# Transposing the routed tokens on VectorE, in blocks of 32, instead of on TensorE

## The chip, the core and the metric

The kernel runs on one core of one Trainium2 chip. The metric is the device time of one execution in microseconds. Three executions of the kernel before took 958.41, 960.04 and 960.34 us; the median is 960.04 us.

## What is computed

There are 4096 tokens (64 x 64) with 512 features each. First every token goes through a conditioning layer: `h = cond_w[itok].T @ x + fside[itok]`, where `itok` names one of 8 subjects for each group of 64 tokens. The reference then computes a mixture of experts on `h`:

- logits `h @ gate_weight.T` over 16 experts, sigmoid, a bias, the best 2 of 4 groups, the best 4 experts of those, and their scores normalized and scaled by 2.5 as weights `w`;
- for each chosen expert `y = silu(h @ gate.T) * (h @ up.T) @ down.T`, with 512 features in and out and 256 hidden ones, added with its weight `w`;
- one shared expert of the same shape for every token, with weight 1;
- the result is `x` + the routed sum + the shared output, all in float32.

## The kernel before, in words

**Tiles.** Work is cut into tiles of 128 tokens (one token per partition). There are NT = 32 tiles of all tokens for the shared expert, and then NR = 143 routed tiles: the (token, expert) pairs sorted by expert, each expert padded to whole tiles. The tile number n runs from 0 to 174 through one software pipeline over both kinds; LAST is 174.

**Stages.** First 32 tiles are conditioned (TensorE, line 697), stored as rows of `h_rows` in HBM and their logits are made (lines 707 to 714). VectorE computes the routing from them beside this stage and beside the 32 shared tiles. Then the 143 routed tiles run. Most of them are in a hardware loop (`run_tiles`, line 90), which is unrolled 16 times; a head and a tail stand outside it.

**Precision.** A float32 product is made of three products in the type fp32r: the operand's high part times the weights' high part, high times low, and low times high (`split_product`, line 770). ScalarE makes a high part by a copy (lines 583, 589 and 608), and VectorE the low part by subtracting it (lines 1204, 1209 and 1236).

**One routed tile n.** GpSimd gathers 128 rows of `h_rows` into a slot of `tok_ring` (line 490); the 8 slots hold 512 features and the token's 16 expert weights. TensorE transposes the features, four blocks of 128x128, into the PSUM bank `psT[n % 2]` (`xpose`, line 747). ScalarE copies that into `xT_hi` (line 583), and VectorE makes `xT_lo` (line 1204). TensorE does the gate and up product, 12 matmuls of 512 columns, into `psGU` (`gate_up`, line 779). ScalarE applies Silu (line 636), and VectorE multiplies by the up half and the expert's weight (`mix`, line 1221). TensorE transposes the hidden values, two blocks, into `psH` (`xpose_hid`), which are split in the same way (lines 589 and 1209), and does the down product, 6 matmuls of 512 columns, into `psY` (`down`, line 787). ScalarE copies this to a slot of `y_ring`, of which there are 4 (line 598). GpSimd adds the rows into `out` by an indirect DMA that accumulates (line 495).

**The order on each engine in pipeline step n.** It is written out by hand, and every engine works in order:

- TensorE: transposes of x of tile n+1, gate and up product of n, hidden transposes of n-1, down product of n-2.
- ScalarE: `copy_y` of n-3, `copy_xT` of n+1, Silu of n, `copy_hidT` of n-1, then up to three pieces of the next expert's weights (line 608).
- VectorE: `split_x` of n+1, `mix` of n, `split_hid` of n-1, then the weights' pieces (line 1236).
- GpSimd: for routed tile r, the gather of r+9 once `mix` has freed its slot, then the scatter of r once SyncE has allowed it.
- SyncE (SP), in its own step n: where the expert table says so, it starts the load of a next expert's weights (1.5 MB, line 380); then it waits until y of n is copied (line 407), waits for earlier scatters where the expert changes (line 411), and allows the scatter (line 412). It runs about three steps behind TensorE, since y of n is copied in ScalarE's step n+3.

**The rings.** `x_ring` (8 slots of 128x512) holds the input of the conditioning stage, and later tables of the routing; in the routed stage it is not used. The expert weights come with their k axis laid out so that feature `k * 128 + p` lies on partition p (`columns`, line 1341).

Of the kernel before, what the change touches and what calls it, by code (L numbers as in the profile page):

```python
# [14 lines left out]
P = 128  # L15
B, C, H = 64, 64, 512
N = B * C
NT = N // P
# [15 lines left out]
YRING = 4  # L34
AHEAD = 9
PAD_SETS = 4
PADS = PAD_SETS * P
# [67 lines left out]
def build(nc, x, itok, fside, cond_w, gate_w, expert_bias, ffn_w, out):  # L105
# [4 lines left out]
    with ExitStack() as ctx:  # L110
# [6 lines left out]
        def sem(name):  # L117
            return ctx.enter_context(nc.semaphore(name))
# [182 lines left out]
        dve_clear = sem("dve_clear")  # L301
        xposed = sem("xposed")
        xT_ready = sem("xT_ready")
        gu_done = sem("gu_done")
# [10 lines left out]
        TURNS = (NR - RING) // (2 * RING) * 2  # L315
        FFN = (0, NT + NR - RING * TURNS - 1, TURNS, 1)
        LAST = NT + NR - 1

# [16 lines left out]
        def is_shared(n):  # L335
            return n is not None and n < NT
# [4 lines left out]
        def _(sp):  # L341
# [35 lines left out]
            def load_raw(turn, odd):  # L377
# [4 lines left out]
                             ).then_inc(raw_loaded, 16)  # L382

            def shared_step(t, n):
                if n in RAW_LOADS:
                    turn = RAW_LOADS[n]
                    if turn == 1:
                        sp.wait_ge(order_ready, 1)
                    else:
                        sp.wait_ge(low_done, PIECES * (turn - 1))  # L390
                        sp.wait_ge(raw_loaded, 16 * (turn - 1))
                    load_raw(turn, turn % 2)
                if n + RING - 1 < NT:
                    load_h(n + RING - 1)
# [18 lines left out]

            def step(t, n, j):
                if is_shared(n):
                    shared_step(t, n)
                else:
                    if n == NT:
                        sp.wait_ge(sp_words_ready, 1)
                    routed_step(t, n)  # L420

            run_tiles(sp, *FFN, step)

# [111 lines left out]
        def _(act):  # L535
# [43 lines left out]
            def copy_xT(t, n):  # L579
                act.wait_ge(xposed, t.done(1))  # L580
                if n is None or n >= 2:
                    act.wait_ge(gu_done, t.done(-1))
                act.activation(xT_hi[:, t.slot % 2, :], psT[t.slot % 2][:], ACT.Copy).then_inc(xhi_ready, 1)  # L583
# [74 lines left out]
        def _(pe):  # L658
# [88 lines left out]
            def xpose(t, n):  # L747
                if is_shared(n):
                    pe.wait_ge(h_loaded[t.slot], (t.rnd + 1) * 16)
                else:  # L750
                    pe.wait_ge(gathered[t.slot], (t.rnd - (NT // RING - 1)) * 16)
                if n is None or n >= 2:
                    pe.wait_ge(xT_ready, t.done(-1))
                transposes(psT[t.slot % 2], tok_ring[:, t.slot, 0:H], HK).then_inc(xposed, 1)
# [57 lines left out]
            def step(t, n, j):  # L812
# [5 lines left out]
                kept.append(at)  # L818
                if n is None or n < LAST:
                    xpose(t + 1, None if n is None else n + 1)  # L820
                gate_up(t, n, kept[-1], needed)
# [22 lines left out]
        def _(v):  # L844
# [357 lines left out]
            def split_x(t):  # L1202
                v.wait_ge(xhi_ready, t.done(1))
                v.tensor_tensor(xT_lo[:, t.slot % 2, :], psT[t.slot % 2][:], xT_hi[:, t.slot % 2, :].bitcast(F32),  # L1204
                                ALU.subtract).then_inc(xT_ready, 1)

            def split_hid(t):
                v.wait_ge(hidhi_ready, t.done(1))
                v.tensor_tensor(hidT_lo[:, t.slot % 2, :], psH[:, 0:I], hidT_hi[:, t.slot % 2, :].bitcast(F32),  # L1209
                                ALU.subtract).then_inc(hidT_ready, 1)  # L1210
# [81 lines left out]
            def step(t, n, j):  # L1292
# [7 lines left out]
                if n is None or n < LAST:  # L1300
                    split_x(t + 1)
                if is_shared(n):
                    route_part(n)
# [25 lines left out]
            split_x(tile_at(0))  # L1329
            run_tiles(v, *FFN, step)  # L1330
            split_hid(tile_at(LAST))


# [34 lines left out]
```

## Time and profile before

| what | value |
|---|---|
| median of three runs | 960.04 us |
| the profiled execution's own time | 958.84 us |
| its span (first to last instruction) | 957.0 us |
| TensorE matmul busy | 935.2 us (98%) |
| VectorE busy | 411.6 us (43%) |
| ScalarE busy | 399.7 us (42%) |
| GpSimd busy | 432.1 us (45%) |
| mean granted TensorE clock | 0.991 |
| queue q0 (GpSimd's DMAs), time of its packets | 50.0% of 16 engines |
| queue q1 (SP's DMAs), time of its packets | 15.3% of 16 engines |

The profiled execution is one run under the hardware profiler. A share of the span is an average over stages with different limits. Matmuls overlap in this view (each is shown for 0.39 us, though the next begins 0.23 us later), so that the length of a stretch is better read from the chain of waits, which is the work that ended last, followed back. A DMA queue's share is the time that its packets took, over all 16 DMA engines.

### The profile page before, as it was taken

What the parts mean: (1) busy time and instruction counts of PE and PEld (TensorE: products, weight loads), DVE (VectorE), ACT (ScalarE), POOL (GpSimd) and SP (SyncE); (2) the same over time, 40 slices, a digit from 0 to 9 for tenths busy, and PEclk for the clock granted to TensorE, in tenths of its full rate; (3) what the DMA queues carried; (4) which work ended last, traced back from release to release, by engine and by line L of the source; (5) the groups of instructions that cost most, each with busy time, mean ns of one, the idle gap of its engine ahead of it and who ended that gap; (6) DMA issues with size and microseconds to landing.
All of it is one profiled execution on the core that took longest, in us unless ns stands there. A gap on an engine that the chain in (4) does not pass through costs nothing.

```text
span 957.0 us, 21289 instructions
## 1 busy us (share of the span) xinstructions
PE 935.2 (98%) x4822; PEld 762.0 (80%) x4823; DVE 411.6 (43%) x930; ACT 399.7 (42%) x852; POOL 432.1 (45%) x402
## 2 busy tenths in 40 slices
PE   7999999999999999999999999999999999999994
PEld 4777887888888888788888888888888878888883
DVE  1375667776343333443234423534435344343331
ACT  3664333443443333443335433534435344344331
POOL 4330211113355555465465555545554646555533
PEclk9998999999999999999999999999999999999997
DMA  7978686867786666577565866686866858666644
GB/s 230 346 242 259 144 170 165 242 119 198 171 187 113 109 114 113 99 201 162 108 119 107 238 122 111 125 232 114 209 146 159 201 94 190 114 112 114 110 66 56
DMA packets 54465, 149.15 MB, mean 156 GB/s; under 512 B 7434, under 2 KB 7442, under 8 KB 51986
## 3 DMA queue, kind: packets, MB, share of 16 engines
q0 software_dynamic: 37296, 86.95, 50.0%
q1 hardware_dynamic: 15586, 50.12, 15.3%
q10 hardware_dynamic: 1408, 10.49, 3.2%
q14 instruction: 155, 1.27, 0.4%
q8 instruction: 20, 0.33, 0.1%
HBM read 90.87 MB, written 65.04 MB: 163 GB/s over the span
## 4 chain that ended last, share of the span: by engine, by line
PE 95%; issue 2%; ACT 0%; POOL 0%; DMA 0%; DVE 0%; DVEq 0%; POOLq 0%; ACTq 0%; SPq 0%
PE psGU L775 50%; PE psY L775 25%; PE psT L672 9%; PE psH L672 4%; PE psY L697 3%; PE psGU L713 3%; PE psM L801 1%; POOL out L495 0%; DMA cond_sb<-cond_w 0%; DVE xT_lo L1204 0%; ACT split_w L608 0%; PE psM L725 0%; POOLq L476 0%; ACT xT_hi L583 0%; PE psM L682 0%
## 5 line engine op out<-in xcount | busy, mean ns | idle before, releaser
L775 PE MATMUL psGU<-split_w,xT_hi 128*128 (+1 forms) x1400 | 450.8, 403 | 2.4 <-DVE xT_lo L1204 2.4
L495 POOL DMA_INDIRECT out<-y_ring,idx_all x143 | 231.0, 1615 | 275.0 <-SPq L412 269.5
L775 PEld LDWEIGHTS psGU<-split_w,xT_hi 128*128 128x128 f32 x1400 | 251.6, 190 | 48.1 <-issue 2.7
L775 PE MATMUL psGU<-split_w,xT_lo 128*128 (+1 forms) x700 | 275.8, 394 | 0.0
L775 PE MATMUL psY<-split_w,hidT_hi 128*128 (+1 forms) x700 | 232.9, 414 | 0.5 <-issue 0.5
L636 ACT ACTIVATE aT<-psGU 128x256 f32<-128x256 f32 x175 | 67.4, 385 | 344.3 <-PE psGU L775 344.3
L1204 DVE TENSOR_TENSOR xT_lo<-psT,xT_hi 128x512 fp32r<-128x512 f32 x175 | 120.8, 690 | 196.6 <-ACT xT_hi L583 195.1
L598 ACT ACTIVATE y_ring<-psY 128x512 f32<-128x512 f32 x175 | 103.9, 594 | 152.6 <-PE psY L775 126.5
L1221 DVE SCALAR_TENSOR_TENSOR aT<-aT,tok_ring,psGU 128x256 f32<-128x256 f32 x143 | 68.8, 481 | 227.5 <-ACT aT L636 227.5
L490 POOL DMA_INDIRECT tok_ring<-h_rows,idx_all x143 | 145.6, 1018 | 46.2 <-issue 42.3
L775 PEld LDWEIGHTS psGU<-split_w,xT_lo 128*128 128x128 f32 x700 | 132.0, 189 | 28.9
L775 PE MATMUL psY<-split_w,hidT_lo 128*128 (+1 forms) x350 | 138.9, 397 | 0.0
L672 PEld LDWEIGHTS psT<-ident,tok_ring 128*128 128x128 f32 x828 | 104.2, 142 | 41.8 <-issue 16.8
L775 PEld LDWEIGHTS psY<-split_w,hidT_hi 128*128 128x128 f32 x700 | 118.6, 189 | 16.7 <-issue 1.0
L672 PE MATMUL psT<-ident,tok_ring 128*128 128x128 f32 x828 | 125.6, 275 | 0.3 <-ACT scores L570 0.3
L583 ACT ACTIVATE xT_hi<-psT 128x512 fp32r<-128x512 f32 x175 | 103.7, 593 | 1.5 <-PE psT L672 1.4
L504 POOL DMA_DIRECT2D out<-y_ring x32 | 27.6, 862 | 153.1 <-ACT y_ring L598 153.1
L775 PEld LDWEIGHTS psY<-split_w,hidT_lo 128*128 128x128 f32 x350 | 65.7, 188 | 14.5
L1209 DVE TENSOR_TENSOR hidT_lo<-psH,hidT_hi 128x256 fp32r<-128x256 f32 x175 | 73.1, 418 | 1.0 <-ACT hidT_hi L589 1.0
L1236 DVE TENSOR_TENSOR split_w<-raw_w,split_w x42 | 51.5, 1226 | 48.8 <-ACT split_w L608 48.3
L589 ACT ACTIVATE hidT_hi<-psH 128x256 fp32r<-128x256 f32 x175 | 66.5, 380 | 1.4 <-PE psH L672 1.4
L672 PEld LDWEIGHTS psH<-ident,aT 128*128 128x128 f32 x350 | 48.6, 139 | 23.0 <-DVE aT L1221 0.4
(170 smaller groups left out, 470.8 us busy)
## 6 DMA issues: line engine op xcount, KB each, us to landing
raw_w<-ffn_w SPq DMA_DIRECT2D x17, 1536.0 KB, 8.2
h_rows<-tok_ring SPq DMA_DIRECT2D x32, 256.0 KB, 3.5
tok_ring<-h_rows SPq DMA_DIRECT2D x32, 256.0 KB, 4.0
out<-y_ring POOLq DMA_DIRECT2D x32, 256.0 KB, 4.6
x_ring<-x SPq DMA_DIRECT2D x24, 256.0 KB, 4.0
tok_ring<-h_rows,idx_all POOLq DMA_INDIRECT x143, 4.4
out<-y_ring,idx_all POOLq DMA_INDIRECT x143, 4.9
x_ring<-x ACTq DMA_DIRECT2D x8, 256.0 KB, 3.7
```

Source lines behind the costliest of these rows:

```text
L490: pool.indirect_dma_start(tok_ring[:, r % RING, :], None, h_rows[:, :], bass.IndirectOffsetOnAxis(idx_all[:, r:r + 1], 0)).then_inc(gather ...
L495: pool.indirect_dma_start(out[:, :], bass.IndirectOffsetOnAxis(idx_all[:, r:r + 1], 0), y_ring[:, r % YRING, :], None, compute_op=ALU.add) ...
L583: act.activation(xT_hi[:, t.slot % 2, :], psT[t.slot % 2][:], ACT.Copy).then_inc(xhi_ready, 1)
L589: act.activation(hidT_hi[:, t.slot % 2, :], psH[:, 0:I], ACT.Copy).then_inc(hidhi_ready, 1)
L598: act.activation(y_ring[:, s, :], psY[t.slot % 2][:], ACT.Copy).then_inc(y_ready, 1)
L636: act.activation(silu[:, t.slot % 2, :], psGU[t.slot % 2][:, 0:I], ACT.Silu).then_inc(silu_ready, 1)
L672: mm = pe.transpose(dst[:, k * P:(k + 1) * P], src[:, k * P:(k + 1) * P], ident[:])
L775: mm = pe.matmul(dst, a[:, slot, c], w(at + col + k * H), start=(k == 0 and a is high and at == 0), stop=(k == parts - 1 and a is low))
L1204: v.tensor_tensor(xT_lo[:, t.slot % 2, :], psT[t.slot % 2][:], xT_hi[:, t.slot % 2, :].bitcast(F32), ALU.subtract).then_inc(xT_ready, 1)
L1209: v.tensor_tensor(hidT_lo[:, t.slot % 2, :], psH[:, 0:I], hidT_hi[:, t.slot % 2, :].bitcast(F32), ALU.subtract).then_inc(hidT_ready, 1)
L1221: ins = v.scalar_tensor_tensor(out=hid[:, half, :], in0=gate, scalar=tok_ring[:, t.slot, bass.ds(expert + H, 1)], in1=up, op0=ALU.mult, op ...
L1236: v.tensor_tensor(low, raw, high.bitcast(F32), ALU.subtract).then_inc(low_done, 1)
```

## The change

For the 143 routed tiles, TensorE's four transposes of x and their waits are gone; the 32 shared tiles keep theirs. In their place stand:

- `shuffle` on SP: per routed tile, four DMAs from `tok_ring` to `x_ring`, all on the chip. DMA number `quad` takes columns `quad*128` to `quad*128+127` of all 128 partitions (512 bytes each) and puts them on the 32 partitions of that quadrant, four tokens side by side on each: token 4b+j goes to partition `32*quad + b`, place j. SP issues those of tile n+6 at the start of its own step n, after it has waited for that tile's gather and, from the ninth on, for the slot of `x_ring` to be free.
- `turn_x` on VectorE: one `transpose` instruction per tile over 128x512, which transposes each block of 32x32 within its quadrant and writes to `psT`. It stands in step n for tile n+2, between `split_x` of n+1 and `mix` of n.
- The features of a partition are then `128*quad + 32*k + a` for partition `32*quad + a`, not `128*k + p`; the routed experts' gate and up weights are laid out to match by the host (`quad_columns`), while the shared expert's and all down weights stay as they were.
- ScalarE's `copy_xT` waits for `turned` instead of `xposed` on routed tiles.
- SP's and VectorE's loops run two rounds fewer and leave 17 steps as a tail instead of one (`EARLY`), since these two engines look ahead.

```diff
@@ -33,6 +33,9 @@
 RING = 8
 YRING = 4
 AHEAD = 9
+SHUFFLE_AHEAD = 6
+QUADS = 4
+Q = P // QUADS
 PAD_SETS = 4
 PADS = PAD_SETS * P
 PIECES = 3
@@ -300,6 +303,8 @@
         act_clear = sem("act_clear")
         dve_clear = sem("dve_clear")
         xposed = sem("xposed")
+        shuffled = [sem(f"shuffled{s}") for s in range(RING)]
+        turned = sem("turned")
         xT_ready = sem("xT_ready")
         gu_done = sem("gu_done")
         silu_ready = sem("silu_ready")
@@ -314,6 +319,7 @@
 
         TURNS = (NR - RING) // (2 * RING) * 2
         FFN = (0, NT + NR - RING * TURNS - 1, TURNS, 1)
+        EARLY = (0, NT + NR - RING * TURNS - 1, TURNS - 2, 1 + 2 * RING)
         LAST = NT + NR - 1
 
         def split_slot(raw_piece, split_piece):
@@ -380,6 +386,17 @@
                 sp.dma_start(raw_w[:, bass.ds(odd * EW, EW)],
                              ffn_w[bass.ds(expert, 1), :, :].rearrange("o p w -> (o p) w")
                              ).then_inc(raw_loaded, 16)
+
+            def shuffle(t, n):
+
+                if n is None or n >= NT + RING:
+                    sp.wait_ge(turned, t.done(1 - NT - RING))
+                    sp.sem_inc(sp_clear, 1)
+                sp.wait_ge(gathered[t.slot], (t.rnd - (NT // RING - 1)) * 16)
+                for quad in range(QUADS):
+                    q = quad * Q
+                    sp.dma_start(x_ring[q:q + Q, t.slot, :].rearrange("b (j e) -> b j e", j=QUADS),
+                                 tok_ring[:, t.slot, quad * P:(quad + 1) * P]).then_inc(shuffled[t.slot], 16)
 
             def shared_step(t, n):
                 if n in RAW_LOADS:
@@ -412,6 +429,9 @@
                 sp.sem_inc(scatter_ok, 1)
 
             def step(t, n, j):
+                m = None if n is None else n + SHUFFLE_AHEAD
+                if m is None or NT <= m <= LAST:
+                    shuffle(t + SHUFFLE_AHEAD, m)
                 if is_shared(n):
                     shared_step(t, n)
                 else:
@@ -419,7 +439,7 @@
                         sp.wait_ge(sp_words_ready, 1)
                     routed_step(t, n)
 
-            run_tiles(sp, *FFN, step)
+            run_tiles(sp, *EARLY, step)
 
         @block.gpsimd
         def _(pool):
@@ -577,7 +597,10 @@
                     copy_x(0)
 
             def copy_xT(t, n):
-                act.wait_ge(xposed, t.done(1))
+                if is_shared(n):
+                    act.wait_ge(xposed, t.done(1))
+                else:
+                    act.wait_ge(turned, t.done(1 - NT))
                 if n is None or n >= 2:
                     act.wait_ge(gu_done, t.done(-1))
                 act.activation(xT_hi[:, t.slot % 2, :], psT[t.slot % 2][:], ACT.Copy).then_inc(xhi_ready, 1)
@@ -745,11 +768,8 @@
                           ).then_inc(sp_words_summed, 1)
 
             def xpose(t, n):
-                if is_shared(n):
-                    pe.wait_ge(h_loaded[t.slot], (t.rnd + 1) * 16)
-                else:
-                    pe.wait_ge(gathered[t.slot], (t.rnd - (NT // RING - 1)) * 16)
-                if n is None or n >= 2:
+                pe.wait_ge(h_loaded[t.slot], (t.rnd + 1) * 16)
+                if n >= 2:
                     pe.wait_ge(xT_ready, t.done(-1))
                 transposes(psT[t.slot % 2], tok_ring[:, t.slot, 0:H], HK).then_inc(xposed, 1)
 
@@ -816,8 +836,8 @@
                     pe.wait_ge(words_ready, 1)
                 at, needed = weights(t, n)
                 kept.append(at)
-                if n is None or n < LAST:
-                    xpose(t + 1, None if n is None else n + 1)
+                if n is not None and n + 1 < NT:
+                    xpose(t + 1, n + 1)
                 gate_up(t, n, kept[-1], needed)
                 if n != 0:
                     xpose_hid(t + -1, None if n is None else n - 1)
@@ -1203,6 +1223,13 @@
                 v.wait_ge(xhi_ready, t.done(1))
                 v.tensor_tensor(xT_lo[:, t.slot % 2, :], psT[t.slot % 2][:], xT_hi[:, t.slot % 2, :].bitcast(F32),
                                 ALU.subtract).then_inc(xT_ready, 1)
+
+            def turn_x(t):
+
+                v.wait_ge(xT_ready, t.done(-1))
+                v.wait_ge(shuffled[t.slot], (t.rnd - (NT // RING - 1)) * 16 * QUADS)
+                v.transpose(psT[t.slot % 2][:].rearrange("p (k b j) -> p k j b", k=HK, j=QUADS),
+                            x_ring[:, t.slot, :].rearrange("p (j k a) -> p k j a", j=QUADS, k=HK)).then_inc(turned, 1)
 
             def split_hid(t):
                 v.wait_ge(hidhi_ready, t.done(1))
@@ -1299,6 +1326,8 @@
                     expert = word & (E - 1)
                 if n is None or n < LAST:
                     split_x(t + 1)
+                if n is None or NT - 2 <= n < LAST - 1:
+                    turn_x(t + 2)
                 if is_shared(n):
                     route_part(n)
                 mix(t, n, expert)
@@ -1327,7 +1356,7 @@
             count_slots(2)
             route_weights(2)
             split_x(tile_at(0))
-            run_tiles(v, *FFN, step)
+            run_tiles(v, *EARLY, step)
             split_hid(tile_at(LAST))
 
 
@@ -1343,11 +1372,18 @@
         e, n, k = w.shape
         return w.transpose(0, 2, 1).reshape(e, k // P, P, n).transpose(0, 2, 1, 3)
 
-    gate = np.concatenate([L0_ffn_gate_proj, np.asarray(L0_ffn_shared_gate)[None]])
-    up = np.concatenate([L0_ffn_up_proj, np.asarray(L0_ffn_shared_up)[None]])
+    def quad_columns(w):
+
+        e, n, k = w.shape
+        return w.transpose(0, 2, 1).reshape(e, QUADS, HK, Q, n).transpose(0, 1, 3, 2, 4).reshape(e, P, HK, n)
+
+    def both(gate, up, order):
+        return np.concatenate([order(np.asarray(gate)), order(np.asarray(up))], axis=3).reshape(-1, P, UP)
+
+    gate_up = np.concatenate([both(L0_ffn_gate_proj, L0_ffn_up_proj, quad_columns),
+                              both(np.asarray(L0_ffn_shared_gate)[None], np.asarray(L0_ffn_shared_up)[None], columns)])
     down = np.concatenate([L0_ffn_down_proj, np.asarray(L0_ffn_shared_down)[None]])
-    ffn_w = np.concatenate([np.concatenate([columns(gate), columns(up)], axis=3).reshape(E + 1, P, UP),
-                            columns(down).reshape(E + 1, P, IK * H)], axis=2)
+    ffn_w = np.concatenate([gate_up, columns(down).reshape(E + 1, P, IK * H)], axis=2)
     arrays = {
         "x": np.ascontiguousarray(x),
         "itok": np.ascontiguousarray(itok_B_0_7),
```

## Rows read from the trace of the kernel before

**Rows 1.** The page: the chain that ended last, by engine.

```profile
PE 95%; issue 2%; ACT 0%; POOL 0%; DMA 0%; DVE 0%; DVEq 0%; POOLq 0%; ACTq 0%; SPq 0%
```

**Rows 2.** The chain of waits, routed stage: start us, us, what.

```profile
599.13 0.44 PE psT L672 x4
599.57 2.76 PE psGU L775 x12
602.33 0.22 PE psH L672 x2
602.54 1.40 PE psY L775 x6
603.94 0.44 PE psT L672 x4
```

**Rows 3.** Windows: us, PE, PEld, DVE, ACT, POOL busy, PEclk, DMA share, GB/s.

```profile
300.00:400.00 100.00, 100.00 (x501) 82.17 (x500) 32.51 (x62) 37.22 (x84) 51.56 (x40) 1.00 0.62 113
```

**Rows 4.** The page's DMA issues: count, KB each, median us to landing.

```profile
tok_ring<-h_rows SPq DMA_DIRECT2D x32, 256.0 KB, 4.0
...
tok_ring<-h_rows,idx_all POOLq DMA_INDIRECT x143, 4.4
out<-y_ring,idx_all POOLq DMA_INDIRECT x143, 4.9
```

**Rows 5.** Waits of TensorE's weight loads, all of the span.

```profile
PEld psT L672 <- issue: 16.8, 61, 0.6
```

**Rows 6.** Timeline of the step that begins at 603.94: start us, us, what.

```profile
604.24 0.58 ACT L598 ACTIVATE y_ring<-psY 128x512 f32<-128x512 f32 x1
...
604.71 0.59 ACT L583 ACTIVATE xT_hi<-psT 128x512 fp32r<-128x512 f32 x1
...
604.99 1.23 DVE L1236 TENSOR_TENSOR split_w<-raw_w,split_w  x1 [1.11 <-ACT split_w L608]
...
606.13 0.68 DVE L1204 TENSOR_TENSOR xT_lo<-psT,xT_hi 128x512 fp32r<-128x512 f32 x1
...
607.77 0.48 DVE L1221 SCALAR_TENSOR_TENSOR aT<-aT,tok_ring,psGU 128x256 f32<-128x256 f32 x1 [0.95 <-ACT aT L636]
607.98 0.98 POOL L490 DMA_INDIRECT tok_ring<-h_rows,idx_all  x1 [0.31 <-issue]
...
608.16 0.42 DVE L1209 TENSOR_TENSOR hidT_lo<-psH,hidT_hi 128x256 fp32r<-128x256 f32 x1
```

**Rows 7.** The page's groups: busy, mean ns | idle before, releaser.

```profile
L1204 DVE TENSOR_TENSOR xT_lo<-psT,xT_hi 128x512 fp32r<-128x512 f32 x175 | 120.8, 690 | 196.6 <-ACT xT_hi L583 195.1
...
L1236 DVE TENSOR_TENSOR split_w<-raw_w,split_w x42 | 51.5, 1226 | 48.8 <-ACT split_w L608 48.3
```

**Rows 8.** Groups of all lines: the shortest VectorE operation over full partitions.

```profile
L1151 DVE MAX8 top<-cond_sb 128x8 f32<-128x16 f32 x32 | 2.5, 147 | 0.0
```

**Rows 9.** Line 380, the weight loads: issue ns, and landing.

```profile
L380 SPq DMA_DIRECT2D raw_w<-ffn_w x16: 346/356/385, 153.3 to 800.6; - x16
...
DMA to landing us min/median/max: 7.2/8.2/12.5
```

**Rows 10.** Waits of SP, 300 to 900 us: total, times, longest.

```profile
SPq L411 <- DMA out<-y_ring,idx_all: 29.5, 13, 5.3
```

**Rows 11.** DMA queues 330 to 390 us, no weight load: packets, MB, share.

```profile
q0 software_dynamic: 2751, 6.57, 61.2%
```

**Rows 12.** DMA queues 418.5 to 425.5 us, during a weight load.

```profile
q1 hardware_dynamic: 132, 1.43, 54.5%
q0 software_dynamic: 296, 0.68, 43.3%
```

**Rows 13.** DMA queues 30 to 50 us: the engines full, rows of 2 KB.

```profile
DMA packets 3017, 7.91 MB, mean 396 GB/s; under 512 B 330, under 2 KB 330, under 8 KB 2886
...
q1 hardware_dynamic: 2438, 5.76, 76.5%
```

**Rows 14.** The one store of 64-byte runs (4096 of them), line 507.

```profile
DMA to landing us min/median/max: 8.5/8.5/8.5
```

## The prediction

> **What bounds the kernel now.** I read the chain of waits first: 95% of the span lies on TensorE [rows 1]. In the routed stage the chain shows one step as four pieces: 0.44 us for the four transposes of x, 2.76 us for the gate and up product, 0.22 us for the hidden transposes, 1.40 us for the down product, and then the next transposes. A step takes 603.94 - 599.13 = 4.81 us, and nothing but TensorE is in it [rows 2]. The windows confirm it: from 300 to 400 us TensorE is busy for all of 100 us at a granted clock of 1.00 (its upper level, 2.4 GHz), VectorE for 32.5, ScalarE for 37.2 and GpSimd for 51.6 us [rows 3]. So the stage is TensorE's, and the DMA engines, at 0.62, are what stands nearest to it. The 143 routed tiles [rows 4] take 143 x 4.81 = 687.8 us of the 958.84 us of the profiled execution; the other 271.0 us aren't touched.
>
> **What is removed.** Four transposes a tile, 0.44 us on the path [rows 2]: 143 x 0.44 = 62.9 us. The piece runs from start to start, so that it holds the change from one kind of weights to the other as well; the matmul that comes first then follows the last one of the down product as every other does, 1.40 / 6 = 0.23 us behind. A step becomes 4.37 us. What comes before a tile's first weight load on TensorE's queue (reading the tile's word, two waits) stays. Today it shows ahead of the transposes' weight load as 16.8 us over 61 steps [rows 5], beside matmuls that cover it. Without the transposes it stands directly before the long ones. It costs nothing if the down product's last matmul covers it, and 16.8 us if all of it comes out. I take 0, as the chain shows no gap at that place now.
>
> **VectorE.** It has today, in a step with a weight piece, 1.23 + 0.68 + 0.48 + 0.42 = 2.81 us [rows 6], and without one 1.58 us; with 42 pieces of 1.226 us [rows 7] over 143 tiles the mean is 1.94 us. That leaves 4.37 - 1.94 = 2.43 us for the transpose, which no row shows. The nearest row is the subtraction over the same 128x512 elements, also with PSUM at one end, 690 ns [rows 7]. From below, 418 ns as for the half as large `hidT_lo` (0.42 us, [rows 6]); from above, as if each of its 16 blocks a quadrant cost what the shortest instruction does, 16 x 147 ns = 2.35 us [rows 8]. I take 0.69. All of this range stays below 2.43. In order of time it fits as well: `split_x` begins 2.19 us into the step that starts at 603.94 and ends at 2.87, `mix` begins at 3.83, and would begin some 0.4 earlier; the transpose fits between, or moves `mix` by 0.2 us. The product of `mix` is wanted by TensorE only after the next gate and up product. So it costs nothing.
>
> The table of the Trainium skill, "VectorE: DVE Perf Modes", section "Rules for kernel authors", advises TensorE for a transpose of 128x128 that ends in PSUM, which is against this change. The trace says otherwise where TensorE is the bound: its 0.44 us a tile are on the chain and VectorE's time isn't. By the figure of that page's section "The three transpose paths" (311 ns for a 128x128 transpose in bf16 on VectorE), an estimate is 4 x 311 = 1.24 us a tile, and the sum would be the same.
>
> **SP.** Four issues a tile. A plain issue takes 356 ns [rows 9], so 1.42 us of 4.37; SP spends its time waiting for y. They stand before that wait, so `scatter_ok` isn't later. What is queued behind SP's new waits (gather landed, slot turned) is `scatter_ok`, and behind that GpSimd's scatter and next gather. The gather of tile k+7 begins 4.04 us into step k [rows 6] and SP wants it at 3 x 4.37 + 0.88 = 13.99: 9.9 us, where it lands in 4.4 [rows 4]. The slot of `x_ring` was read six steps before.
>
> **The new chain.** y of tile k-3 is copied 0.88 us into step k (0.30 + 0.58, [rows 6]). Then SP issues the four transfers of tile k+4, until 2.3. A plain 256 KB load lands after 4.0 us [rows 4], I take that for these: 6.3. VectorE wants them in step k+2 at 2 x 4.37 + 2.87 = 11.6, so 5.3 us are spare. If they come later, VectorE stands still with `mix` and `split_hid` behind it, and TensorE stalls only if `hidT_lo` is late for the down product at 3 x 4.37 + 2.98 = 16.1, so if the transfers land after 16.1 - 0.42 - 0.48 - 0.69 = 14.5. Two things can use that up. The transfers share SP's queue with the 1.5 MB weight loads, 12 in the stage (16 [rows 9] less the four issued in shared steps): behind one that takes 8.2 us to land they land at about 10.2, behind the worst of 12.5 us [rows 9] at 14.5. And the wait for scatters at an expert's change holds SP for 29.5 / 13 = 2.3 us, at worst 5.3 [rows 10]. Both worst ones together are 5.3 us too late: between 0 and 12 x 5.3 = 64 us. I take 3 us.
>
> **DMA engines.** Without a weight load GpSimd's queue takes 61.2% of 60 us, for 60 / 4.81 = 12.5 tiles: 2.94 us a tile, for 0.526 MB [rows 11]. During a weight load the same queue moves 0.68 MB in 43.3% of 7 us, 4.46 us per MB, so 2.34 us a tile; both queues together are at 98% there, so that is its time when the engines are full [rows 12]. A weight load takes 54.5% of 7 us for 1.43 MB, 4.2 us for 1.57 MB, which is 12 x 4.2 / 143 = 0.35 us a tile. New are 4 x 128 packets of 512 bytes, 32 for each of 16 engines. No row shows such a packet. From below by bytes: 5.76 MB in 76.5% of 20 us [rows 13] is 23.5 GB/s an engine, 22 ns. From above: 4096 runs of 64 bytes landed in 8.5 us with all that it takes [rows 14], 256 an engine, 33 ns each, and 19 ns for 448 bytes more: 52 ns. Further above still: any packet as the mean one of SP's queue with the engines full, 15.3 us x 16 / 2438 = 100 ns [rows 13]. I take 40 ns, between the two bounds that fit the size: 1.28 us a tile. The sum is 2.34 + 0.35 + 1.28 = 3.97 us, below 4.37, so the engines carry it, at some nine tenths. With 52 ns it is 4.36, right at the limit, with 66 ns it is the 4.81 us of before.
>
> **The sum.** 958.84 - 62.9 + 3 = 898.9 us for an execution like the profiled one. The median of the runs shown lies 1.2 us above that one, so I forecast 900 us.
>
> **Rivals.**
>
> - *The DMA engines become the bound; slower.* For it speaks that the queue of GpSimd is at 0.62 already and that 512 new packets a tile are twice the 256 of gather and scatter. With GpSimd's queue at its full 2.94 us and 52 ns a packet a step takes 2.94 + 0.35 + 1.66 = 4.95 us: 271.0 + 143 x 4.95 = 979 us; with 100 ns a packet, 2.34 + 0.35 + 3.2 = 5.89 us, 1113 us. It decides against the change from 66 ns a packet on. Against it: during a weight load the engines move 1.43 + 0.68 MB in 7 us, 301 GB/s, beside the same scatters [rows 12]. The Trainium skill, "DMA: Bandwidth & Descriptors", section "Bandwidth", speaks for it: it measures 0.95 us for a 64 KB transfer and calls small ones bound by descriptors. An estimate from that figure would be 3.8 us a tile for the four if they didn't overlap, and 6.5 us a step, 1199 us in all; no run so far shows that size.
> - *Stalls around weight loads.* Each of 12 loads costs some 2.6 us, half of the worst, or a wait for gathers on SP delays scatters and these the ring of y: 31 us, so 930 us; at the worst the gain is gone. For it: the load itself takes up to 12.5 us to land [rows 9], and gathers and scatters share the engines with it.
> - *TensorE's own queue shows.* The 16.8 us come out: 916 us.
> - *The change doesn't do what it says.* The removed 0.44 us is replaced by another wait of TensorE in every step, such as a VectorE transpose over 2.43 us; with a step of 4.81 us again, 960 us, and each 0.1 us more costs 14 us.
>
> **Chances.** The forecast with small stalls or the queue's (892 to 918): 0.65. Stalls around loads (918 to 958): 0.17. No change: 0.03. DMA-bound or VectorE-bound and slower: 0.15. Below about 0.2%, 2 us, this kernel's measurement tells nothing. Faster 0.82, same 0.03, slower 0.15. The range from 892 to 950 us leaves out the slower rival and the last of the stalls, some 0.19.
>
> **What would show it.** Right: 4.37 us between two gate and up products in the chain, with no piece of `psT` between; TensorE busy all of 100 us; the transpose at about 0.7 us; the share of SP's queue up by 1.28 / 4.37 = 29% of the routed stage, a total of 0.9 or less; SP's waits still mostly on y. Wrong: DMA at a full share with 200 MB/s no higher, landings of gathers over 9.9 us, VectorE's transpose released by a DMA with `mix` late behind it, TensorE waiting for `xT_lo` or `hidT_lo`. If the packets take over 66 ns, the sign is wrong.

## The result

The changed kernel takes 1018.86 us (median of four executions, 1015.38 to 1019.52), against 959.9 us before: a ratio of 1.061, 95% interval 1.0583 to 1.0636. It is slower by 59 us, where 60 us less was forecast. The profiled execution has a span of 1013.6 us.

The page of the profile after, its lines for TensorE, for the chain of waits and for the new instruction:

```profile
PE 913.5 (90%) x4250; PEld 714.1 (70%) x4251; DVE 495.3 (49%) x1073; ACT 412.6 (41%) x852; POOL 431.2 (43%) x402
...
DMA 31%; PE 27%; SPq 26%; issue 14%; ACT 0%; ACTq 0%; POOL 0%; DVE 0%; POOLq 0%; DVEq 0%
DMA out<-y_ring,idx_all 28%; SPq L398 15%; PE psGU L795 10%; PE psY L795 6%; SPq L414 5%; PE psY L720 3%; PE psT L695 3%; PE psGU L736 3%; SPq L427 2%; DMA x_ring<-tok_ring 2%; PE psH L695 1%; PE psM L821 1%; DMA out<-y_ring 1%; SPq L428 1%
...
L1231 DVE STREAM_TRANSPOSE psT<-x_ring 128x512 f32<-128x512 f32 x143 | 103.6, 724 | 261.3 <-DMA x_ring<-tok_ring 242.2
```

TensorE holds 27% of the chain, where it had 95% [rows 1]. In its place stand SP's instruction queue (SPq), the time between instructions ("issue") and DMA. The DMA share has to be read with care. It is nearly all the landing of scatters (28%), put down as what released line 428, SP's wait for earlier scatters. The chain takes any landing that falls just before such a wait for its end. In 43 of the 65 pieces of this kind (181 of 286 us) SP came to line 428 less than 0.1 us after its instruction before, so that nothing held it there. The windows (columns as in [rows 3]) show TensorE idle for 14 of 100 us, where it had no idle time, and that the DMA engines aren't full:

```profile
600.00:700.00 100.00, 85.86 (x364) 64.30 (x364) 47.68 (x82) 42.64 (x84) 47.09 (x37) 0.97 0.80 177
```

The chain of waits from 602 to 608 us, one step of SP (start us, us, what), answers to [rows 2]:

```profile
602.72 0.02 SPq L429
...
602.85 0.55 SPq L398
603.40 0.05 issue
603.45 0.60 SPq L398
604.05 0.04 issue
604.09 0.60 SPq L398
604.69 0.04 issue
604.73 0.60 SPq L398
...
605.48 1.04 SPq L414
...
606.55 0.04 SPq L417
...
606.89 0.02 SPq L424
...
607.59 0.02 SPq L429
```

Line 429 allows a scatter; from one to the next 4.87 us pass, and in them SP waits for nothing. (It is one of the shorter steps; the median plain one takes 4.96 us.) Four issues of transfers (L398) with the gaps behind them take 0.64 us each, 2.5 us together; the read of the tile's word (L414) takes 1.04 us; the rest, some 1.3 us, is register arithmetic and semaphore instructions of 17 to 80 ns with about 50 ns between them. The wait for y (L424) takes no time. SP's waits from 300 to 900 us in the kernel before had, beside [rows 10],

```profile
SPq L407 <- ACT y_ring L598: 338.7, 111, 7.0
```

and the whole-span list of after has

```profile
SPq L428 <- DMA out<-y_ring,idx_all: 12.9, 22, 1.2
...
SPq L424 <- ACT y_ring L621: 6.3, 4, 3.8
```

So SP has become the engine that hardly ever waits. Who waits for it, by the list of waits (total us, times, longest):

```profile
POOL out L515 <- SPq L429: 332.9, 139, 6.3
DVE psT L1231 <- DMA x_ring<-tok_ring: 242.2, 97, 7.9
...
ACT xT_hi L606 <- DVE psT L1231: 106.8, 53, 6.3
```

VectorE's transpose waits for transfers that SP issues late, ScalarE's copy waits for the transpose, and TensorE for both.

I added up SP's instructions from one line 429 to the next, between 330 and 900 us of the trace after. Means:

| SP's steps | count | us each |
|---|---|---|
| plain | 90 | 5.09 (median 4.96) |
| with the issue of a weight load | 9 | 6.53 |
| with a turn of the hardware loop | 4 | 8.30 |
| with both | 2 | 9.19 |
| all | 105 | 5.41 |

In the kernel before a step has 4.83 us in this count, of which SP works about 1.45 in a plain step. Some plain steps hold a short standstill of SP at line 428 (the 22 in the list above, 1.2 us at most), which is why their mean is above their median. TensorE's steps, from one Silu of ScalarE to the next over the 143 routed tiles, have 5.24 us on the mean, where they had 4.82: 142 x 0.42 = 59 us, the whole loss. (The mean of 5.41 above is of 330 to 900 us alone.) Their median is only 4.59 us: TensorE's loss comes in bunches of up to 13 us, with shorter steps between, while SP goes on at its own pace.

### The profile page after: what moved, and what is told of

Same layout as the page of the kernel before. It is cut to its first block, busy times and chain, and to the rows that moved or that the text cites. A ratio compares the mean times of both kernels' runs of the same rounds, so it can differ in the third digit from the quotient of the medians.

```text
span 1013.6 us, 21153 instructions
## 1 busy us (share of the span) xinstructions
PE 913.5 (90%) x4250; PEld 714.1 (70%) x4251; DVE 495.3 (49%) x1073; ACT 412.6 (41%) x852; POOL 431.2 (43%) x402
## 4 chain that ended last, share of the span: by engine, by line
DMA 31%; PE 27%; SPq 26%; issue 14%; ACT 0%; ACTq 0%; POOL 0%; DVE 0%; POOLq 0%; DVEq 0%
DMA out<-y_ring,idx_all 28%; SPq L398 15%; PE psGU L795 10%; PE psY L795 6%; SPq L414 5%; PE psY L720 3%; PE psT L695 3%; PE psGU L736 3%; SPq L427 2%; DMA x_ring<-tok_ring 2%; PE psH L695 1%; PE psM L821 1%; DMA out<-y_ring 1%; SPq L428 1%; SPq L386 1%
## 5 line engine op out<-in xcount | busy, mean ns | idle before, releaser
L515 POOL DMA_INDIRECT out<-y_ring,idx_all x143 | 226.9, 1586 | 334.1 <-SPq L429 332.9
L795 PEld LDWEIGHTS psGU<-split_w,xT_hi 128*128 128x128 f32 x1400 | 265.0, 194 | 100.7 <-issue 45.2
L795 PE MATMUL psGU<-split_w,xT_lo 128*128 (+1 forms) x700 | 278.7, 398 | 0.0
L795 PE MATMUL psY<-split_w,hidT_hi 128*128 (+1 forms) x700 | 239.9, 424 | 4.1 <-issue 4.1
L1231 DVE STREAM_TRANSPOSE psT<-x_ring 128x512 f32<-128x512 f32 x143 | 103.6, 724 | 261.3 <-DMA x_ring<-tok_ring 242.2
L795 PEld LDWEIGHTS psGU<-split_w,xT_lo 128*128 128x128 f32 x700 | 134.9, 193 | 29.7
L795 PEld LDWEIGHTS psY<-split_w,hidT_hi 128*128 128x128 f32 x700 | 122.3, 193 | 24.9 <-issue 6.0
L695 PE MATMUL psH<-ident,aT 128*128 128x128 f32 x350 | 69.2, 279 | 49.0 <-DVE hidT_lo L1236 35.1
L695 PEld LDWEIGHTS psH<-ident,aT 128*128 128x128 f32 x350 | 44.8, 142 | 86.0 <-DVE aT L1248 48.2
L1248 DVE SCALAR_TENSOR_TENSOR aT<-aT,tok_ring,psGU 128x256 f32<-128x256 f32 x143 | 63.9, 447 | 24.2 <-ACT aT L659 16.5
```

Of the source, the lines that this page charges most:

```text
L515: pool.indirect_dma_start(out[:, :], bass.IndirectOffsetOnAxis(idx_all[:, r:r + 1], 0), y_ring[:, r % YRING, :], None, compute_op=ALU.add) ...
L695: mm = pe.transpose(dst[:, k * P:(k + 1) * P], src[:, k * P:(k + 1) * P], ident[:])
L795: mm = pe.matmul(dst, a[:, slot, c], w(at + col + k * H), start=(k == 0 and a is high and at == 0), stop=(k == parts - 1 and a is low))
L1231: v.transpose(psT[t.slot % 2][:].rearrange("p (k b j) -> p k j b", k=HK, j=QUADS), x_ring[:, t.slot, :].rearrange("p (j k a) -> p k j a", ...
```

## Experiments

Theory S: SP's own stream of instructions is the bound. Theory D: the transfers cost it, by the time of the DMA engines or by landing late. Theory C: scatters run one after another through SP. Two more theories, from e6_earlier on, are on what stays above the 900 us of the forecast once SP is relieved. Theory L: transfers that land late, behind or beside weight loads. Theory F: the turns of the hardware loop. All runs below are compared with runs of the kernel before on the same chip.

**e1_half: two of the four transfers left out.**

```diff
-                for quad in range(QUADS):
+                for quad in range(QUADS // 2):
...
-                v.wait_ge(shuffled[t.slot], (t.rnd - (NT // RING - 1)) * 16 * QUADS)
+                v.wait_ge(shuffled[t.slot], (t.rnd - (NT // RING - 1)) * 32)
```

> The changed kernel with two of the four transfers left out (quadrants 2 and 3 of x_ring keep old data, so half of the transposed x is left uncomputed). Theory S (SP's own instruction stream is the bound: 4.87 to 4.99 us a step without a wait, four issues at 0.64 us each): an SP step falls to 4.95 - 1.28 = 3.67 us, TensorE's 4.37 us is the bound again, 895 to 915 us. Theory D (the transfers themselves, by their time on the DMA engines or by how late they land): half the packets are gone, so about half of the loss against 900 comes back, 950 to 975 us. Theory C (scatters are serialized, each waits on SP for the one before to land): no change, 1010 to 1025 us.

928.77 us, ratio 0.968 (0.9643 to 0.971). The median step of TensorE is 4.35 us, as forecast for a kernel that TensorE bounds, but the mean is 4.64. S in its direction, with 14 us more than it allowed; C falls. D isn't excluded by this one.

**e2_word_first: the read of the word ahead of the transfers.**

```diff
-                word = sp.value_load(sp_word[0:1, bass.ds(t.done(-NT), 1)])
...
+                    word = sp.value_load(sp_word[0:1, bass.ds(t.done(-NT), 1)])
                 if m is None or NT <= m <= LAST:
                     shuffle(t + SHUFFLE_AHEAD, m)
...
```

> The changed kernel with SP's read of the tile's word ahead of the four transfers in each step, instead of behind them, where it takes 1.04 us and not 0.27 as before. Nothing else moves. Theory S: an SP step falls from 4.95 to about 4.19 us, below TensorE's 4.37, with more in steps that load weights: 900 to 940 us. Theories D and C: unchanged, 1010 to 1025 us.

968.61 us, ratio 1.0084 (1.0054 to 1.0113). Moving one instruction, with every DMA as it was, gives back 50 us; D and C have no room for that. S's range was missed by 29 us. The step of 4.19 us that it rested on is reached only by the shortest plain steps of SP (4.14 us and a little more); the median plain step takes 4.50 us and the mean of all 5.08. Between its instructions SP stands for some 0.36 us in many steps and up to 1.7 us for a scatter in some, and single issues take 0.8 to 2.0 us. The read itself, in nanoseconds (min/median/max), in the changed kernel and here:

```profile
L414 SPq TENSOR_LOAD <-sp_word x105: 270/1022/1199, 333.5 to 896.2; - x105
```

```profile
L435 SPq TENSOR_LOAD <-sp_word x112: 262/277/867, 333.2 to 898.6; - x112
```

Three quarters of a microsecond a step were the price of standing behind four issues. Behind two it costs next to nothing, as e1_half shows, where the read is still in its old place:

```profile
L414 SPq TENSOR_LOAD <-sp_word x122: 47/274/1245, 333.3 to 897.4; - x122
```

**e3_two_on_act: two transfers from SP, two from ScalarE's queue.**

```diff
-                for quad in range(QUADS):
+                for quad in range(QUADS // 2):
...
+                m = None if n is None else n + ACT_AHEAD
+                if m is None or NT <= m <= LAST:
+                    shuffle_rest(t + ACT_AHEAD, m)
...
-            run_tiles(act, *FFN, step)
+            run_tiles(act, *EARLY, step)
```

> The changed kernel with two of the four transfers of a tile issued from ScalarE's queue (in its gap behind the copy of xT) and two from SP. The same packets, the same bytes. Theory S: SP at 3.67 us a step, ScalarE at some 3.5 us, so TensorE's 4.37 us is the bound: 895 to 915 us. Theory D: the same transfers cost the same, 1000 to 1025 us. Theory C: 1010 to 1025 us.

940.7 us, ratio 0.9787 (0.9745 to 0.9829): the same transfers, and 78 us less than the changed kernel, 20 us less than before. S has the direction, and its range of 895 to 915 us was missed by 26 us. The median step is 4.34 us, and from 800 to 900 us, where only the last weight load is issued (at 801.6), TensorE has no hole, with the DMA engines fuller than in the changed kernel:

```profile
800.00:900.00 100.00, 100.00 (x463) 81.96 (x463) 53.82 (x98) 44.27 (x98) 61.36 (x47) 1.00 0.95 203
```

D is refuted as the main cause: the same packets move here, and the engines carry more in the same time. The Trainium skill, "Trainium Kernel Development and Optimization", section "Key Constraints", says that DMAs from several queues run on the same 16 engines and that issuing from several only saves the sequencer's issue time. The trace agrees: that saving is what was missing here.

**e4_before_idle: the kernel before, with the four transfers of each tile read by nobody.**

```diff
             def step(t, n, j):
+                m = None if n is None else n + SHUFFLE_AHEAD
+                if m is None or NT <= m <= LAST:
+                    shuffle(t + SHUFFLE_AHEAD, m)
...
+                if r >= RING:
+                    pool.wait_ge(shuffled[r % RING], r // RING * 16 * QUADS)
...
```

> The kernel before, with the four transfers of each routed tile issued by SP in the same place as in the changed kernel, but read by nobody; TensorE keeps its transposes. Only GpSimd's gather into the same slot eight tiles later waits for them. Theory S: SP's step of 4.95 us and more is longer than TensorE's 4.81, so nearly the whole time of the changed kernel comes back without the rest of the change: 1000 to 1030 us. Theory D by late landing: nobody waits for the data, 958 to 965 us. Theory D by full DMA engines: also near 1015 us.

1009.3 us, ratio 1.0534 (1.0499 to 1.0568), inside S. TensorE's transposes are all there, and no engine waits for the data but GpSimd's gather eight tiles later, and still 49 of the 59 us are lost. SP's step is 5.34 us on the mean. The way to TensorE is another one: late scatters, then no free slot of y for ScalarE, a wait that the kernel before doesn't list:

```profile
ACT y_ring L621 <- DMA out<-y_ring,idx_all: 208.2, 77, 9.2
```

**e5_both: e3_two_on_act with the read ahead of SP's two transfers.**

```diff
-                for quad in range(QUADS):
+                for quad in range(QUADS // 2):
...
-                word = sp.value_load(sp_word[0:1, bass.ds(t.done(-NT), 1)])
...
+                    word = sp.value_load(sp_word[0:1, bass.ds(t.done(-NT), 1)])
...
+                    shuffle_rest(t + ACT_AHEAD, m)
...
```

> Two transfers of a tile from ScalarE's queue and two from SP (as in e3_two_on_act), and SP's read of the word ahead of its two. Theory S (SP's instruction stream was the bound) says that nothing is left to win there: the median step of e3_two_on_act is 4.34 us, TensorE's own, and the word costs SP 0.32 us in it. So 935 to 945 us, as e3_two_on_act (940.7). If SP's stream still bounds some steps, 920 to 935.

945.69 us, ratio 0.9837 (0.9804 to 0.9871). No gain, as S says of a queue that is no longer the bound; it lies 0.7 us above the upper end that was expected. With two issues ahead the read takes 0.279 us in the median in e3_two_on_act already, so there was little to move.

**e6_earlier: e5_both with all transfers one step earlier.**

```diff
-SHUFFLE_AHEAD = 6
-ACT_AHEAD = 4
+SHUFFLE_AHEAD = 7
+ACT_AHEAD = 5
```

(The values of e5_both are on the lines with a minus.)

> e5_both with the transfers of a tile issued one step earlier on both queues (SHUFFLE_AHEAD 7 for 6, 5 for 4 on ScalarE). Theory L (what is left above 900 us are steps in which the transfers land late, behind or beside a weight load): one step more of lead, 4.4 us, takes most of it away: 910 to 925 us. Theory F (what is left are the loop's turns, at which ScalarE and VectorE stand 4 to 7 us for their next instructions, where it was 3 to 4.5 us before): no change, 935 to 945 us. Slower if the gathers aren't there yet one step earlier.

965.59 us, ratio 1.0064 (1.0038 to 1.009): slower than e5_both by 20 us. The time in which ScalarE's Silu is held up by its own queue, where the new waits for the gather now stand, rises from 118.3 us in e5_both to

```profile
ACT aT L675 <- issue: 191.2, 82, 9.2
```

Directly ahead of ScalarE's issues of transfers, the first of which waits for the gather, 38 standstills over 0.2 us add up to 70 us, where e5_both has 9 with 11 us. So the gathers aren't there a step earlier, and a wait in ScalarE's queue holds up everything behind it. This is the "slower" that the expectation allowed for. It shows that the lead can't be had in this way, and leaves open what it would have won: theory L isn't decided by it.

**e7_small_loads: e3_two_on_act with 12 small weight loads.**

```diff
...
-                    load_raw(turn + 2, turn & 1)
+                    load_raw(turn + 2, turn & 1, P)
...
```

> e3_two_on_act, but the 12 weight loads of the routed stage bring 128 of 3072 columns each (the rest of the weights stays old, so that the routed sums are not the reference's). Every wait and every split stays. Theory L: the whole excess is the loads': 900 to 910 us. Theory F: the turns of the loop cost 3.7 us each or less without the load beside them, as in the kernel before, of which a part shows: 910 to 925 us.

911.8 us, ratio 0.9504 (0.9469 to 0.954). Of the 41 us between e3_two_on_act and the forecast of 900, 29 go with the bytes of the weight loads, 2.4 us each, beside the transfers, gathers and scatters. Which wait they lengthen isn't shown. The 12 us that stay fit the loop's turns: of the ten longest gaps between two Silus, nine lie within 10 us of one of ScalarE's six turns. That is nearness in time and no proof; e10_unroll4 tries it.

**e8_one_plain: one transfer of 128 x 2048 bytes a tile, from SP.**

```diff
-                for quad in range(QUADS):
-                    q = quad * Q
-                    sp.dma_start(x_ring[q:q + Q, t.slot, :].rearrange("b (j e) -> b j e", j=QUADS),
-                                 tok_ring[:, t.slot, quad * P:(quad + 1) * P]).then_inc(shuffled[t.slot], 16)
+                sp.dma_start(x_ring[:, t.slot, :], tok_ring[:, t.slot, 0:H]).then_inc(shuffled[t.slot], 16)
...
```

> The changed kernel with one transfer per tile in place of four, issued by SP in the same place: 128 partitions x 2048 bytes, straight from tok_ring to x_ring without spreading (so the transposed blocks are not the ones wanted). The same bytes, one issue, long runs. Theory S: SP's step falls under 3 us; TensorE's step is the bound; with what the loads and the loop's turns cost (28 to 40 us in e1_half and e3_two_on_act) 910 to 940 us. An issue should take about 0.33 to 0.36 us if the 0.60 us come from the shape (32 partitions x 4 runs of 512 bytes), 0.60 if from SBUF to SBUF; and the read of the word 0.27 to 0.4 us if its 1.04 us come from the four issues ahead of it.

928.38 us, ratio 0.9676 (0.9642 to 0.971), inside S: the same bytes in one issue, and SP waits for y again. The issue takes 0.465 us in the median, between the two guesses, and the read of the word behind this one issue 0.270:

```profile
L396 SPq DMA_DIRECT2D x_ring<-tok_ring x121: 3/465/693, 330.7 to 890.8; - x121
```

```profile
L411 SPq TENSOR_LOAD <-sp_word x123: 15/270/946, 331.3 to 899.0; - x123
```

**e9_after_small_loads: the changed kernel with small weight loads.**

```diff
...
-                    load_raw(turn + 2, turn & 1)
+                    load_raw(turn + 2, turn & 1, P)
```

> The changed kernel (four transfers on SP), but the 12 weight loads of the routed stage bring 128 of 3072 columns each (the rest of the weights stays old). Every wait stays. Theory S says that SP's step of 4.95 us stands on its own: 271 + 143 x 4.95 = 979 us, and some us more for the loop's turns, 980 to 995 us; the rest of the changed kernel's 1019 us is the loads'. If most of the loss were the loads' (as 29 of the 40 us in e3_two_on_act), 930 to 960 us.

1018.3 us, ratio 1.0616 (1.0597 to 1.0635). No change at all, and the expected 980 to 995 was wrong. I had taken the 0.46 us between SP's median and mean step for waits on transfers. It is instructions, loop turns and short standstills: the steps of SP with a load still take 6.52 us with a twenty-fourth of a load's bytes. The bytes of the loads cost time with SP relieved (e7) and none with SP as the bound, where their instructions do.

**e10_unroll4: e3_two_on_act with half the loop turns.**

```diff
-    unroll = 2
+    unroll = 4
...
-        EARLY = (0, NT + NR - RING * TURNS - 1, TURNS - 2, 1 + 2 * RING)
+        EARLY = (0, NT + NR - RING * TURNS - 1, TURNS - 4, 1 + 4 * RING)
...
```

> e3_two_on_act with the loop unrolled 32 steps a turn instead of 16 (3 or 4 turns instead of 6 to 8, on every engine). Theory F: a turn costs the standstill of ScalarE's and VectorE's instruction queues, some 2 to 3 us each, so 6 to 10 us come back: 930 to 936 us. If the turns are hidden or code has to be fetched all the same: 938 to 944 us, as e3_two_on_act (940.7).

938.79 us, ratio 0.9781 (0.976 to 0.9803); e3_two_on_act has 0.9787, and their intervals overlap. Nothing is won: three steps near the turns that are left are now 11.2 to 13.8 us long, where single ones were up to 9.3. So a lower number of turns doesn't give back the 12 us, and what they are stays open. It is the fastest complete version of this study, by no margin over e3_two_on_act.

**e11_reads_only: twelve more reads on SP in the kernel before.**

```diff
+                for _ in range(12):
+                    sp.value_load(sp_word[0:1, 0:1])
```

> The kernel before, with nothing of the change, and twelve more reads of a word into a register on SP at the start of each routed step; no DMA is added and nothing waits for them. Theory S: SP's own work in a step of the kernel before ends 1.45 us after y is copied; with 12 x 0.31 us it is 5.2 us in a plain step, above TensorE's 4.81, and steps with a weight load or a turn of the loop come on top, as in the changed kernel (5.41 on the mean against 4.95 in the median there): 5.2 to 5.65 us a step, 1010 to 1080 us. Theory D (DMA engines or transfers): no transfer is added, 958 to 965 us.

961.0 us, ratio 1.0006 (0.9987 to 1.0025). It says nothing on the theories: the profile has one read a step, the others are not in the compiled program.

**e12_sp_work_only: 56 increments on SP in the kernel before, no DMA.**

```diff
+                for _ in range(56):
+                    sp.sem_inc(sp_clear, 1)
```

> The kernel before, with nothing of the change and no DMA added: SP increments a semaphore that nobody waits for 56 times at the start of each routed step (the twelve reads of e11_reads_only were left out by the compiler, so that one tested nothing). An increment takes 17 ns and comes 67 ns behind the one before it, so 3.7 us more on SP; with its own 1.45 us a plain step of SP is 5.2 us, above TensorE's 4.81. Theory S: SP is the bound; at least 143 x (5.2 - 4.81) = 56 us more, and steps with weight loads and loop turns on top as in the changed kernel: 1010 to 1080 us. Theory D (DMA engines, late landings): nothing is transferred, 958 to 965 us.

1180.62 us, ratio 1.2308 (1.2279 to 1.2337), 100 us more than the upper end that was expected. SP now also stands between two increments for 0.4 us on the mean some 220 times in 89 steps, about 1 us a step, which the sum hadn't; why it stands isn't shown. SP's step is 6.44 us: 271 + 143 x 6.44 = 1192 us by S's sum, 1180.6 measured. The DMA engines are less busy than in the kernel before in the same stretch (0.53 against 0.68):

```profile
300.00:900.00 600.00, 492.65 (x2278) 391.25 (x2276) 171.31 (x312) 184.50 (x406) 249.47 (x187) 0.96 0.53 108
```

and the waits are those of e4_before_idle:

```profile
ACT y_ring L600 <- DMA out<-y_ring,idx_all: 543.3, 127, 9.3
...
POOL out L497 <- SPq L414: 493.9, 142, 6.3
```

SP's instructions alone, without any of the change and without a transfer, slow the kernel. With the trace of the changed kernel, in which SP hardly waits, and with e2_word_first, which gives back most of the loss with every transfer kept, this shows the cause: SP's stream of instructions.

## Why the prediction was wrong

- **What bounds the kernel before, and the 0.44 us: right.** With SP relieved, the median step is 4.34 or 4.35 us (e1, e3, e8), against 4.37 forecast. The two complete kernels that spread the issues (e3, e10) are 2% faster than the kernel before.
- **VectorE: right.** The transpose takes 724 ns (0.69 was taken), and most of its own waiting was for its data (242.2 us, 97 times).
- **SP: the step that failed.** The text costed "Four issues a tile. A plain issue takes 356 ns [rows 9], so 1.42 us of 4.37; SP spends its time waiting for y." The issue takes 0.602 us plus 0.04 behind it, so 2.5 us. The read behind them went from 0.27 to 1.02 us. And SP's own work in a step, 1.45 us with its gaps, was in the trace and not in the sum. 2.5 + 0.75 + 1.45 = 4.7 us, and the two new waits with their arithmetic make 4.87 to 4.96. That alone is past TensorE's 4.81. "They stand before that wait, so `scatter_ok` isn't later" fell with it: it holds only while a wait is left to stand before. On top come 1.4 us in steps with a weight load and 3.2 us at each turn of the loop (8.30 less 5.09), which the wait for y had hidden.
- **SP's waiting time was read as room for one term.** In a plain step SP works 1.45 us, so 4.81 - 1.45 = 3.4 us were free before, and 4.37 - 1.45 = 2.9 after. (On the mean of all steps it is less: it waited 338.7 us for y in 600, 2.7 us a step.) The four issues at their true price with the dearer read are 3.3. No rival took SP's own instructions for the bound, and so none had their price.
- **DMA engines: right that they carry it, and cheaper than taken.** From 330 to 390 us of the trace after (packets, MB, share), which answers to [rows 11]:

```profile
q0 software_dynamic: 2640, 6.27, 58.9%
q1 hardware_dynamic: 6652, 3.03, 18.2%
```

  0.182 x 60 us x 16 / 6652 = 26 ns a packet, near the lower bound of 22; 40 was taken. The sign of being wrong at 66 ns a packet didn't come, and the kernel is slower all the same. The rival that the DMA engines become the bound had the sign of the result but not its mechanism: e3 runs the same packets in 940.7 us.
- **Stalls around weight loads: under-sized, and hidden in this kernel by the larger loss.** 3 us were taken; with SP relieved they are 29 us (e3 against e7). That this is near the 31 us of the rival proves nothing for its mechanism, as no run shows which wait the loads lengthen. In the changed kernel itself the bytes of the loads cost nothing (e9).
- **"TensorE's own queue shows": not as told, and on a misread row.** All 16.8 us of [rows 5] lie before 300 us, in the stages that keep their transposes; from 300 us on the transposes' weight loads have no such wait, and the list of after still has 16.3 us in 61 for them. With SP relieved the routed stage has no such wait in every step, but 9 (e1) or 8 (e3) longer ones ahead of the gate and up product, 20 us in all, whose end the profile doesn't tell.
- **"The change doesn't do what it says": no.** The 0.44 us are gone from TensorE's step, as the medians of e1 and e3 show, and no fixed wait stands in their place.
- **TensorE or VectorE for the transpose: rightly decided.** That the Trainium skill, "VectorE: DVE Perf Modes", section "Rules for kernel authors", advises TensorE for such a transpose was put aside for a right reason: VectorE, with 724 ns a tile, wasn't what made this slow. The price lay in bringing the data into its quadrants.

## What to carry to other kernels

A queue that only issues and waits has a time per step too: add up its instructions and the gaps between them, at the price of the shape that is to be issued, and compare that sum with the step after the change, before reading its idle time as room. What stands behind a burst of issues on the same queue can get dearer, as the read did here behind four; put reads and grants ahead of it. Check a long share of landings in a chain of waits against the gap before the instruction that they are said to release. If an issuing queue is the bound, spread the issues over a second queue first, and expect that a wait placed there holds up whatever that engine computes.

## What the runs showed of the hardware

- An issue on SP took 0.602 us in the median for 32 partitions x 4 runs of 512 bytes from SBUF to SBUF, 0.465 for 128 runs of 2048 bytes from SBUF to SBUF, and 0.356 for the 1.5 MB load from HBM [rows 9].
- A read of one word into a register of SP took 1.02 us in the median behind four issues, 0.274 (e1) and 0.279 (e3) behind two, 0.270 behind one (e8), and 0.277 with none directly ahead (e2). Why isn't shown; in 10 of 105 steps of the changed kernel it took under 0.5 us behind four as well.
- Semaphore increments of 17 ns on SP came some 60 ns apart, with standstills between them.
- A turn of the hardware loop held SP for 2.4 to 5.4 us in the kernel before, which hides it behind the wait for y, and for 2.5 to 4.1 in the changed one. The cause isn't shown.
- TensorE's granted clock lies at its upper level (1.00, 2.4 GHz) from 90 to 940 us of the kernel before. In the changed one it falls to the lower level (0.50, 1.2 GHz) twelve times between 400 and 900 us, for 3.4 or 6.8 us, 55 us in all. Two examples of what TensorE did before: from 482 to 487 us it was busy for 1.7 of 5 us, and from 652 to 657.6 for 2.2 of 5.6. At the lower level one matmul follows the other after 0.43 us, at the upper after 0.23. TensorE was busy for 45 of the 55 us, so an estimate of what the lower level cost TensorE is half of that, 23 us. Little of it can be in the loss: SP, which sets the pace, waited for y for only 6.3 us in the whole changed kernel.
